# Graph attention layer on one core: phase one and the first step put in another order on every engine

## The reference

```python
mask = adj.astype(jnp.float32) + jnp.eye(n, dtype=jnp.float32)
q = (h @ Wq.T + bq).reshape(n, N_HEADS, D_K)
k = (h @ Wk.T + bk).reshape(n, N_HEADS, D_K)
v = (h @ Wv.T + bv).reshape(n, N_HEADS, D_K)
scores = jnp.einsum('nhd,mhd->hnm', q, k) / jnp.sqrt(jnp.float32(D_K))
scores = jnp.where(mask[None, :, :] == 0, jnp.float32(-1000000000.0), scores)
attn = jax.nn.softmax(scores, axis=-1)
ctx = jnp.einsum('hnm,mhd->nhd', attn, v).reshape(n, D_MODEL)
attn_out = ctx @ Wo.T + bo
h1 = _layer_norm(h + attn_out, ln1_g, ln1_b)
ff = jax.nn.relu(h1 @ W1.T + b1) @ W2.T + b2
h2 = _layer_norm(h1 + ff, ln2_g, ln2_b)
```

## Time and profile before

| | |
|---|---|
| median of 3 runs | 555.47 us (554.21 to 555.52) |
| span of the profiled execution | 554.5 us (its own time is this span; nothing else of it is listed) |
| PE busy | 483.4 us, 87% |
| DVE busy | 425.2 us, 77% |
| ACT / POOL busy | 214.5 us (39%) / 262.3 us (47%) |
| transferred | 140.94 MB, mean 254 GB/s |

### The profile page before, as it was taken

The page is one execution under the profiler, slowest core; times in us unless marked ns, Lnnn a source line. Parts: engine busy times, 40 slices in busy tenths (PEclk is TensorE's granted clock), DMA queues, the critical chain, the costliest instruction groups (busy, mean ns, idle before and its releaser), DMA issues.

```text
span 554.5 us, 7282 instructions
## 1 busy us (share of the span) xinstructions
PE 483.4 (87%) x2274; PEld 376.7 (68%) x2274; DVE 425.2 (77%) x978; ACT 214.5 (39%) x526; POOL 262.3 (47%) x381
## 2 busy tenths in 40 slices
PE   5999999757699899799989989979878888789994
PEld 4888888655458757675875776668435767458883
DVE  0648696998979999999999987869988898550103
ACT  1244343324362463345336255423443143532430
POOL 6444347363633556745754553515625555305133
PEclk9999989999699999989989999978788799799998
DMA  7999868999999798998898785344765842401011
GB/s 278 418 417 418 318 214 330 400 409 420 398 329 351 266 366 261 366 348 287 323 348 318 247 292 187 138 165 148 262 222 163 302 143 58 134 1 39 0 39 42
DMA packets 39771, 140.94 MB, mean 254 GB/s; under 512 B 4904, under 2 KB 16552, under 8 KB 35632
## 3 DMA queue, kind: packets, MB, share of 16 engines
q1 hardware_dynamic: 24608, 95.03, 45.3%
q0 software_dynamic: 13328, 43.55, 22.7%
q10 hardware_dynamic: 1792, 1.85, 1.0%
HBM read 123.61 MB, written 16.80 MB: 253 GB/s over the span
## 4 chain that ended last, share of the span: by engine, by line
PE 51%; DVE 19%; DMA 10%; issue 8%; ACT 6%; POOL 5%; SPq 0%; POOLq 0%; ACTq 0%; DVEq 0%
PE ps L1086 15%; PE ps L1099 12%; PE ps L1719 10%; DVE found L504 6%; DMA xT_all<-in_xT 4%; PE ps L843 2%; PE ps L1066 2%; DMA work<-q_table,row_of 2%; POOL slots L1011 2%; DMA adj_buf<-in_adj 2%; PE ps L846 1%; ACT xT_all L1143 1%; PE ps L1076 1%; DMA early<-in_wqkvT 1%; PE ps L1054 1%
## 5 line engine op out<-in xcount | busy, mean ns | idle before, releaser
L504 DVE FIND_INDEX8 found<-ones,adj_buf 128x8 uint32<-128x4105 int32 (+5 forms) x40 | 138.7, 3467 | 0.0
L1086 PE MATMUL ps<-xT_all,w 128*128 128x512 f32 (+1 forms) x288 | 125.7, 585 | 0.3 <-ACT xT_all L1116 0.2
L1099 PE MATMUL ps<-w,xT_all 128*128 128x256 f32 x512 | 122.7, 395 | 2.9 <-ACT xT_all L1133 1.6
L1099 PEld LDWEIGHTS ps<-w,xT_all 128*128 128x128 f32 x512 | 99.2, 199 | 17.7 <-ACT xT_all L1133 2.7
L1086 PEld LDWEIGHTS ps<-xT_all,w 128*128 128x128 f32 x288 | 56.0, 203 | 47.6 <-issue 44.1
L1011 POOL DMA_INDIRECT slots<-kv_table,col_of x54 | 55.9, 1035 | 48.3 <-DVE col_of L587 36.4
L1133 ACT ACTIVATE xT_all<-ps,col_table 128x512 f32<-128x512 f32 (+1 forms) x72 | 45.8, 642 | 57.1 <-PE ps L1086 52.3
L1719 PE MATMUL ps<-early,xT_all 128*128 128x256 f32 x256 | 60.2, 398 | 6.1 <-DMA early<-in_wqkvT 6.1
L1719 PEld LDWEIGHTS ps<-early,xT_all 128*128 128x128 f32 x256 | 50.7, 200 | 14.2 <-DMA xT_all<-in_xT 4.7
L1153 DVE BATCH_NORM_STATS2 stats<-ps 128x6 f32<-128x256 f32 x62 | 22.1, 418 | 36.5 <-PE ps L1054 36.5
L954 ACT ACTIVATE xT_all<-ps,col_table 128x256 f32<-128x256 f32 (+1 forms) x38 | 14.5, 432 | 84.5 <-PE ps L846 84.5
(11 more groups left out here) (180 smaller groups left out, 821.7 us busy)
## 6 DMA issues: line engine op xcount, KB each, us to landing
adj_buf<-in_adj SPq DMA_DIRECT2D x31, 2048.0 KB
xT_all<-in_xT SPq DMA_DIRECT2D x14, 512.0 KB, 24.5
kv_table<-slots POOLq DMA_DIRECT2D x7, 1024.0 KB, 11.2
slots<-kv_table SPq DMA_DIRECT2D x12, 512.0 KB
q_table<-slots POOLq DMA_DIRECT2D x16, 256.0 KB
out_dram<-early SPq DMA_DIRECT2D x7, 512.0 KB
q_own<-q_table SPq DMA_DIRECT2D x12, 256.0 KB
slots<-in_adj SPq DMA_DIRECT2D x1, 2048.0 KB, 23.0
```

The lines of the kernel that those rows point to most:

```text
L504: last = nc.vector.max_index(dst, ones8[:], part)
L1086: last = nc.tensor.matmul(ps[:, q["bank"] + f % 2, 0:q["g"] * P], w1[:, k, f * P:(f + 1) * P], q["h1T"][:, k, :], start=(k == 0), stop=(k ...
L1099: nc.tensor.matmul(to, q["ffT"][:, f, j * P:(j + 1) * P], w2[:, f, :], start=(f == 0), stop=False)
```

## The change

Ahead of the first weights PE runs two matmuls on a tile filled with ones (`WARM`, after one DVE fill). Pair 0 does the keys of both tiles before the values of both (`first_kv`). Query pair 0 is projected, copied and stored after all keys and values instead of after pair 13. Gathers of keys wait for the key tables alone (`keys_ready`), gathers of queries also for the queries (`queries_ready`). Only 4 query pairs instead of 6 go ahead of step 0, and 8 instead of 6 into it. The fifth adjacency is loaded ahead of step 0's own rows. On DVE the searches are no longer tied to pairs, step 0 computes own scores before edge scores, and tile 0's columns and one-hot rows come after them. On ACT the distances of step 1 come before step 0. In the general path, one semaphore does the work of two.

```diff
+        warm = scores0[:, 2 * BANK:3 * BANK]
+        WARM = 2
         def lists_pe(pe, q):
             pe.wait_ge(rt_ready, q.p + 1)
-            pe.wait_ge(distance, 2 * q.p + 2)
+            pe.wait_ge(distance, 2 * (STEPS[1].p if q.first else q.p) + 2)
...
-        def tables_ready(eng, q):
+        def keys_ready(eng):
             for i in range(STAGES):
                 eng.wait_ge(s_kv_out[i], (GROUPS // STAGES if i < STAGES - 1 else GROUPS // STAGES - 1) * 16)
-                if q.first:
-
+            eng.wait_ge(s_kv_last, 2 * 16)
+
+        def queries_ready(eng, q):
+            if q.first:
+                for i in range(STAGES):
                     eng.wait_ge(s_q_out[i], PAIRS // STAGES * 16)
-
-            eng.wait_ge(s_kv_last, 2 * 16)
             pair = (q.no + q.T - 1) // 2
             eng.wait_ge(s_q_out[pair % STAGES], (pair // STAGES + 1) * 16)
...
-        Q_BEFORE = 6
+        Q_BEFORE = 4
         def q_pairs(i, gap):
             if i == 0:
-                return ((6,), (), (7, 8), (9, 10), (11,), ())[gap]
+                return ((), (4, 5), (6, 7, 8), (9, 10), (11,), ())[gap]
...
+            load_adj(sp, 4)
             load_own(sp, STEPS[0])
             sp.wait_ge(got_edges[STEPS[0].par], 2 * STEPS[0].U * 16)
-            load_adj(sp, 4)
             load_adj(sp, 5)
...
+                for p in q_pairs(i, 1):
+                    store_q(p)
                 if soon:
                     gather_edges(pool, soon)
...
             for i in range(PAIRS):
+                if i == PAIRS - 1:
+                    store_kv(PAIRS - 2)
                 take_kv(i)
...
-                if i == 13:
-                    take_q(0)
+            store_kv(PAIRS - 1)
+            take_q(0)
             distance_act(act, TILE0)
-            store_kv(PAIRS - 2)
-            store_kv(PAIRS - 1)
             mask_act(act, TILE0)
+            distance_act(act, STEPS[1])
...
+            def first_kv():
+                order = [(j, part) for part in range(2) for j in range(2)]
+                for j, part in order:
+                    if (j, part) == (0, 0):
+                        pe.wait_ge(s_first_xT, 16)
+                    if j == 0:
+                        pe.wait_ge(s_wqkv[1 + part], 16)
...
+            pe.wait_ge(warm_ready, 1)
+            for _ in range(WARM):
+                nc.tensor.matmul(ps[:, ELL, :], warm[:, 0:P], warm, start=True, stop=True)
+            first_kv()
+            for i in range(1, PAIRS):
                 project_kv(i)
...
-                if i == 13:
-                    project_q(0)
             starts_pe(pe, TILE0)
-            for i in range(1, 4):
-                project_q(i)
-            lists_pe(pe, TILE0)
-            for i in range(4, Q_BEFORE):
+            for i in range(Q_BEFORE):
                 project_q(i)
             starts_pe(pe, b1_)
+            lists_pe(pe, TILE0)
...
+            nc.vector.memset(warm, 1.0).then_inc(warm_ready, 1)
+            dve.wait_ge(s_const, CONSTS)
+            find_dve(dve, b0, 0)
+            find_dve(dve, b0, 1)
+            listed_dve(dve, b0)
+            spill_dve(dve, b0)
+            for us in ((13,), (12,)):
+                find_dve(dve, TILE0, 0, us)
+            rt_dve(dve, b0)
...
-                edge_scores_dve(dve, q)
-                own_scores_dve(dve, q)
+                if i == 0:
+                    own_scores_dve(dve, q)
+                    edge_scores_dve(dve, q)
+                    cols_dve(dve, TILE0)
+                    onehot0_dve(dve)
+                else:
+                    edge_scores_dve(dve, q)
+                    own_scores_dve(dve, q)
```

More of the change, by code:

```diff
@@ L280, in build @@
         s_const = sem("s_const")
+        warm_ready = sem("warm_ready")
         s_wqkv = [sem(f"s_wqkv{i}") for i in range(3)]
@@ L993, in gather_aligned @@
                 pool.wait_ge(aligned_ready, total_prepared(lambda p: 1 if p.nu > 1 and p.A else 0, q.p + 1))
-            tables_ready(pool, q)
+            keys_ready(pool)
             pool.wait_ge(s_pad, 2 * 16)
@@ L1016, in gather_queries @@
             pool.wait_ge(row_ready, q.b + 1)
+            queries_ready(pool, q)
             for u in range(q.U):
@@ L1022, in load_own @@
         def load_own(sp, q):
-            tables_ready(sp, q)
+            keys_ready(sp)
+            queries_ready(sp, q)
             wait(sp, acc_ps, q.before)
@@ L1650, in _ @@
                     post_act_x(act, JOBS[GROUPS], 0)
-                if i + 1 < NB:
+                if 0 < i < NB - 1:
                     distance_act(act, STEPS[i + 1])
@@ L1710, in project_kv @@
                     c, r = (2 * i + j) // GROUP, (2 * i + j) % GROUP
-                    if i == 0 and j == 0:
-                        pe.wait_ge(s_first_xT, 16)
                     if r == (2 if c == 0 else 0):
@@ L1715, in project_kv @@
                     for part in range(2):
-                        if i == 0 and j == 0:
-                            pe.wait_ge(s_wqkv[1 + part], 16)
                         for k in range(KC):
@@ L1720, in project_kv @@
                                                     wqkv[:, k, (1 + part) * D:(2 + part) * D], start=(k == 0), stop=(k == KC - 1))
+                last.then_inc(s_kv_ps, 1)
+            def first_kv():
[5 more added lines that the diff above has]
+                        pe.wait_ge(s_wqkv[1 + part], 16)
+                    for k in range(KC):
+                        last = nc.tensor.matmul(ps[:, kv_bank(0, part), j * D:(j + 1) * D], xT_all[:, 0, k, j * P:(j + 1) * P],
+                                                wqkv[:, k, (1 + part) * D:(2 + part) * D], start=(k == 0), stop=(k == KC - 1))
                 last.then_inc(s_kv_ps, 1)
@@ L1741, in _ @@
             b0, b1_ = STEPS[0], STEPS[1]
-            for i in range(PAIRS):
+            pe.wait_ge(warm_ready, 1)
[3 more added lines that the diff above has]
+            for i in range(1, PAIRS):
                 project_kv(i)
@@ L1828, in _ @@
             b0, b1_ = STEPS[0], STEPS[1]
-            pieces0 = ((13,), (12,), (11,), (10,), (9,), (8, 7), (6, 5), (4, 3), (2, 1, 0))
-            for i in range(PAIRS):
-                if i == 1:
-                    dve.wait_ge(s_const, CONSTS)
-                    find_dve(dve, b0, 0)
-                if i == 3:
-                    find_dve(dve, b0, 1)
-                    listed_dve(dve, b0)
-                    spill_dve(dve, b0)
-                if i == 6:
-                    rt_dve(dve, b0)
-                if 5 <= i <= 13 and pieces0[i - 5]:
-                    find_dve(dve, TILE0, 0, pieces0[i - 5])
-                if i == 10:
-                    cols_dve(dve, b0)
-                if i == 13:
-                    listed_dve(dve, TILE0)
-                    spill_dve(dve, TILE0)
+            nc.vector.memset(warm, 1.0).then_inc(warm_ready, 1)
[7 more added lines that the diff above has]
+            rt_dve(dve, b0)
+            for us in ((11,), (10,), (9,), (8,)):
+                find_dve(dve, TILE0, 0, us)
+            cols_dve(dve, b0)
+            for us in ((7, 6), (5, 4), (3, 2), (1, 0)):
+                find_dve(dve, TILE0, 0, us)
+            listed_dve(dve, TILE0)
+            spill_dve(dve, TILE0)
+            find_dve(dve, b1_, 0)
             starts0_dve(dve)
-            find_dve(dve, b1_, 0)
-            rt_dve(dve, TILE0)
             find_dve(dve, b1_, 1)
-            cols_dve(dve, TILE0)
-            onehot0_dve(dve)
             listed_dve(dve, b1_)
             spill_dve(dve, b1_)
+            rt_dve(dve, TILE0)
             for q in STEPS:
```

10 lines of the change are left out of this document (5 added, 5 removed).

## The result

The changed kernel takes 562.97 us in the median of 4 runs (559.41 to 564.68), the kernel before 555.5 beside it (554.21 to 559.98): ratio 1.0109, 95% interval [1.0056, 1.0161]. The forecast was 550.5, so it missed by 12.5 us and had the sign wrong. Run again in a later job, the changed kernel gave 1.0104 [1.0055, 1.0153].

What follows compares the result with a forecast made beforehand. It took a chain of latencies between phase one and step 0, then DVE's pace beside crowded transfers, as the bounds. Gains of 3.8 us by step 0's end and 1.2 after made 5.0 off 555.5: 550.5 us, range 549 to 552.

Steps and rivals of the forecast that it cites:

- (a): Start of phase one on PE: warm matmuls and keys first let pair 2 start at 16.2, gaining 1.1 us.
- (b): Phase one on PE: query pair 0 behind pair 15 takes 2.2 us off the keys' path; keys end at 65.2.
- first rival: The clock falls in PE's new gap before pair 2, giving 552.2 to 553.5 us; chance 0.20.
- (c): DVE's order ahead of step 0: third search ends at 65.7, DVE ready for step 0 near 75.5.
- (d): Gathers waiting for keys alone: first gather at 74.0, step 0's edges at 83.5, 3.1 us earlier.
- the bound of 6.4 us for the store: Upper end for ACT's last keys-and-values store beside the fifth adjacency: 2.5 us of delay on 3.9; 1.5 taken.
- tables: Rival: fifth adjacency delays ACT's last store, even turns making 3.9 us 7.8; 552.9 us, chance 0.12.
- (e): Step 0 on DVE: 21.2 us from edges to end instead of 21.9, ending at 104.7, 3.8 us earlier.
- 0.5 us for the lists: Low-clock allowance in step 0 for two query pairs on PE ahead of the lists DVE wants: 0.5 us.
- (f): Transfer crowd after 86 us, 2 MB less: xT load lands at 122 to 126, DVE's wait shrinks, 1.2 us gained.
- I let it through whole: After 150 us: the order is unchanged, so the whole 5.0 us gain reaches the end.
- second rival: ACT's queue holds up the exponential DVE needs in step 0: 555 us, or 560.5 at worst; chance 0.08.

Runs made afterwards that it cites:

- q_before: Changed kernel with six query pairs ahead of step 0 again, fifth adjacency still early: 559.8 us, ratio 1.0056 to the kernel before.
- after: First profile of the changed kernel, of its fastest run: 559.41 us.
- again: Second profile of the unaltered changed kernel, of a run of 564.5 us.
- adj_late: Changed kernel with the fifth adjacency put back behind the wait for step 0's gathers: median 556.71 us, ratio 0.9936 to the kernel before.
- best_new_q: best_again with the changed kernel's order of query pairs (4 ahead of step 0): 558.39 us, ratio 1.0068 to the kernel before.
- both_back: Changed kernel with fifth adjacency behind step 0's gathers and six query pairs ahead of step 0: median 554.95 us, ratio 0.9960 to the kernel before.
- late_cols_first: both_back with tile 0's columns and one-hot rows also back ahead of step 0's scores: 553.3 us, ratio 0.9945 to the kernel before.
- before_adj_early: Kernel before with only the fifth adjacency's load moved up, ahead of step 0's own rows: ratio 0.9967 to the kernel before.
- best_again: late_cols_first without the DVE fill and warm matmuls, run once more: 550.44 us, ratio 0.9906 to the kernel before.
- best_adj_early: best_again with the fifth adjacency ahead of step 0's own rows again: 555.03 us, ratio 0.9989 to the kernel before.

## Why the prediction was wrong, step by step

**(a) Right in its gain, wrong in leaving the clock out.** With the clock held, the last copy was at 65.36 against a forecast of 65.2 (for (a) and (b) together). It fell in most profiles and put it at 67.43. That was the first rival; it had 0.20, and the clock fell in 9 of the 15 profiles with such a gap. "Gain 1.1 us, and the same if the clock comes up some us late" looked at the start and not at the gap. The 2.93 us at 232 us were one gap that went well; of two gaps of equal length one may cost 2 us and the other nothing.

**(b), (c) Right, with misses.** The third search ended at 68.8 and 67.1 in the two profiles for 65.7, in the first partly for a DVE instruction of tile 0 that took 1.34 us for 0.4. So the adjacency left only just ahead of the last store. DVE was ready for step 0 at 77.8 for 75.5, still ahead of the gathers.

**(d) The step that failed first: the bound of 6.4 us for the store.** I took it as "the shortest of POOL's seven in a crowd", on the reasoning that a stretch with a share of 0.21 is nearly free. But the 2 MB load that fills it was the change itself. The store took 9.3, 9.7 (q_before), 11.5, 9.5 and 9.9 us in the five profiles in which the load leaves 0.6 to 1.0 us ahead of it, and 2.8 to 4.0 in all others. The earlier trace rows had a warning at hand: a median of 11.2 and a maximum of 16.9, if for stores of twice the size, in a crowd. In "after", edges are 6.75 us later than forecast: the store left 2.2 late (the clock), landed 3.9 later than the 5.4 allowed, and the gathers took 0.7 more. In "again", 0.15 late and 6.1. The rival "tables" named the mechanism and had 0.12, with even turns giving 7.8. All five are worse than even turns. The store ended with the load or behind it, as if it got hardly any of the engines while that ran: the adjacency, issued at 68.81, landed 9.0 later at 77.8, the store at 79.1. The Trainium skill, "DMA: Bandwidth & Descriptors", section "Queues, rings and completion order", has the turns taken a packet at a time; a load of 16 KB rows and a store of 2 KB ones need not share evenly under it. No run here varied the sizes of the rows, so that stays open.

Without the early load the rest of (d) was right: first gather 72.17 to 72.53 with the clock held, where 71.5 + 1.0 was forecast with no delay.

**(e) The second failure: 0.5 us for the lists, the term for the low clock.** The idle time was forecast well: where the load is out of the way, PE is idle 4.74 us for "some 5" (in the changed kernel 10.88, as the gathers are late). What it costs wasn't. A query pair is 2.17 us of PE at full pace (b), so the two ahead of the lists are 4.3, about the 4.1 us of columns that DVE does meanwhile. They took 7.2 us (92.92 to 100.13), 2.9 more, and that is most of the 3.34 that DVE waits. In adj_late it is the same after the shorter idle time:

```profile
85.70 1.10 PE L820 MATMUL ps<-work 128*128 128x56 f32 x4 [4.74 <-DVE work L613]
86.59 2.03 PE L1753 MATMUL ps<-early,xT_all 128*128 128x256 f32 x4
93.20 0.51 PE L808 MATMUL ps<-idx_all,work 128*128 128x9 f32 x4
```

Where no columns stand beside the pairs, their full-pace work is paid as well (best_new_q, 5.54). The wait of 1.18 for the transposed maxima wasn't in the forecast either. Three pairs stand ahead of them in the changed kernel, 6.5 us, but with two (q_before) the wait is 1.30, so their number alone is not the cause; these two took about as long, starting at half pace (2.06 us for four rows). Together 3.34 + 1.18 = 4.5 for 0.5, and step 0 took 25.2 us for 21.2. The other terms hold: the wait of 2.90 went and the own scores were hidden.

**The 4.1 us of columns moved into step 0** were priced right as work, but the place they came from had become idle. Putting them back is worth 1.3 us of step 0 (both_back 107.47, late_cols_first 106.14, both with the clock fallen), and step 0 ends a little over 1 us later than the 104 to 105 expected.

**(f) Right in size, but that may be luck.** The xT load landed in 15.7 us for 20.6, 4.9 less where 5 was forecast. But with the adjacency back in the crowd it took 16.8 (adj_late) and 17.0 (both_back) too, and 18.3 with it out (before_adj_early), so the missing 2 MB aren't shown to be the reason. Issued at 117.3 for 109.5, it came back at 133.0. DVE's 1.52 us became 0.78.

**"I let it through whole" was about right.** Step 0's end 3.9 us earlier than before's in best_again gives a median 5.2 lower; 8.1 us later in best_new_q gives 8.0 more; 2.2 us later in best_adj_early, though, gives 4.6 more. A second rival, the exponential waiting behind ACT's copies, never showed in DVE's waits of the changed kernel.

## What to carry to other kernels

A transfer brought forward into a quiet stretch is itself the crowd there: look at what latency-bound store or gather leaves within a few us of it, and bound that one by the middle and the longest of the rows from a busy stretch, not the shortest of them. Filler work inside a wait cost nothing here, even at half pace; moved behind the wait it was paid, at half pace, and ahead of what the other engine wanted next. Price such work at half pace (2.03 us for 1.03), not with a small allowance. Before moving work off a path, list what its engine does in the hole that it leaves.

## What the runs showed of the hardware

- A 0.5 MB store beside a 2 MB load that left 0.6 to 1.0 us earlier on another queue landed in 9.3 to 11.5 us for 2.8 to 4.0; the last of six small gathers beside such a load landed in 8.2 for 4.1.
- With a gap of TensorE of 1.5 to 2.7 us that ends at 16, the granted clock over 10 to 20 us was 0.83 to 0.87 in 9 profiles (gaps of 1.95 to 2.66) and 1.00 in 6 (1.48 to 2.67); the fall costs 1.4 to 2.1 us. About the same gap, in the same kernel, went either way (2.64 fell, 2.53 held).
- After 4.74, 9.39 and 10.88 us idle and one short group of matmuls, the next four rows on TensorE took 2.03 us for 1.03: half pace, alike after all three (adj_late, best_new_q, changed).
- Chunk 1 of xT lands 13.2 to 13.6 us after its issue whatever TensorE does, so that two warm matmuls brought nothing in any pair of kernels.
- Medians of the kernel before in five jobs went from 555.5 to 557.4; differences under 0.3% between kernels of different jobs were not read.
